# Rounding the feed-forward weights inside the first attention, by sign and comparison

## The reference

```python
def _weight_quant(w):
    scale = 1.0 / jnp.clip(jnp.mean(jnp.abs(w)), 1e-05)
    wq = jnp.clip(jnp.round(w * scale), -1.0, 1.0) / scale
    return w + jax.lax.stop_gradient(wq - w)
def _bitlinear(x, w):
    return jnp.einsum('bsd,fd->bsf', _act_quant(x), _weight_quant(w))
...
x = x + _L0_xattn_ref(_layernorm(x), ctx_512, Wq, Wkv_expand, Wout)
x = x + _L0_ffn_ref(_layernorm(x), W1, W2)      # silu(bitlinear(x, W1)), then bitlinear with W2
x = x + _L1_xattn_ref(_layernorm(x), ctx_512, ...)
x = x + _L1_ffn_ref(_layernorm(x), ...)
```

## Time and profile before

| what | value |
|---|---|
| time, median of 3 runs | 1128.49 us (1125.04 to 1131.27) |
| the profiled execution's own time | 1127.68 us |
| its span, first to last instruction | 1125.9 us |
| busy PE, DVE, ACT, POOL | 88%, 68%, 58%, 25% |
| mean granted TensorE clock | 0.95 of full |

### The profile page before, as it was taken

The page is one execution under the profiler, slowest core; times in us unless marked ns, Lnnn a source line. Parts: engine busy times, 40 slices in busy tenths (PEclk is TensorE's granted clock), DMA queues, the critical chain, the costliest instruction groups (busy, mean ns, idle before and its releaser), DMA issues. The chain is left out here.

```text
span 1125.9 us, 20668 instructions
## 1 busy us (share of the span) xinstructions
PE 994.8 (88%) x7516; PEld 782.9 (70%) x7516; DVE 763.1 (68%) x1654; ACT 651.4 (58%) x1691; POOL 283.4 (25%) x276
## 2 busy tenths in 40 slices
PE   5799999997129999886999999899998999999586
PEld 5678888876014555534888888788887888888485
DVE  6757666664757998435676767577775767777466
ACT  4657777765547878454555555355554555555275
POOL 5765565343033332021001010010101001000372
PEclk9989999999659999987999999999999999999889
DMA  7210000000438000141000000000000000000013
GB/s 263 98 67 6 7 2 2 2 1 1 149 105 249 1 1 2 38 169 57 1 1 19 2 20 2 3 20 1 20 1 23 1 1 1 1 1 2 0 39 113
DMA packets 20091, 41.95 MB, mean 37 GB/s; under 512 B 1168, under 2 KB 4496, under 8 KB 19472
## 3 DMA queue, kind: packets, MB, share of 16 engines
q1 hardware_dynamic: 19984, 40.53, 10.8%
HBM read 36.33 MB, written 4.19 MB: 36 GB/s over the span
## 5 line engine op out<-in xcount | busy, mean ns | idle before, releaser
L1214 POOL TENSOR_TENSOR c_ctx_raw<-c_ctx_raw,c_table 128x1024 f32<-128x1024 f32 x8 | 19.0, 2379 | 448.7 <-PE c_bank_b L1358 366.5
L1440 ACT ACTIVATE probs<-c_score,c_neg_max 128x256 f32<-128x256 f32 x256 | 119.2, 480 | 15.4 <-DVE c_neg_max L1501 15.4
L1426 ACT ACTIVATE c_h<-c_bank_b 128x512 fp32r<-128x512 f32 x64 | 38.3, 598 | 153.6 <-PE c_bank_b L1358 153.6
L559 POOL TENSOR_TENSOR a_probs<-a_probs,a_inv 128x256 f32<-128x256 f32 (+1 forms) x128 | 102.7, 830 | 90.5 <-DVE a_inv L660 90.4
L451 ACT ACTIVATE a_probs<-a_s,a_neg_max 128x128 f32<-128x128 f32 (+1 forms) x256 | 104.4, 435 | 32.3 <-DVE a_neg_max L648 31.9
L1491 DVE TENSOR_TENSOR c_l<-c_bank_b,c_h 128x512 fp32r<-128x512 f32 x64 | 44.3, 692 | 99.2 <-ACT c_h L1426 99.2
L1431 ACT ACTIVATE c_pT_h<-c_turn 128x512 fp32r<-128x512 f32 x128 | 69.9, 596 | 63.4 <-PE c_turn L1348 63.4
L44 PE MATMUL c_acc<-VO_h,c_l 128*128 128x512 f32 x256 | 100.9, 394 | 1.9 <-DVE c_l L1491 1.9
L46 PE MATMUL c_acc<-VO_h,c_h 128*128 128x512 f32 x256 | 100.5, 393 | 0.0
L45 PE MATMUL c_acc<-VO_l,c_h 128*128 128x512 f32 x256 | 100.0, 391 | 0.0
L1501 DVE TENSOR_REDUCE c_neg_max<-c_score 128x2 f32<-128x512 f32 x128 | 82.0, 682 | 9.7 <-PE c_score L1337 8.8
(11 more groups left out here) (253 smaller groups left out, 2866.6 us busy)
## 6 DMA issues: line engine op xcount, KB each, us to landing
w_raw<-in_w SPq DMA_DIRECT2D x1, 4096.0 KB, 13.8
w_raw<-in_w SPq DMA_DIRECT2D x4, 1024.0 KB, 8.8
wq<-in_wq SPq DMA_DIRECT2D x1, 4096.0 KB, 22.8
c_ctx_raw<-in_ctx SPq DMA_DIRECT2D x8, 512.0 KB, 3.6
wo<-in_wo SPq DMA_DIRECT2D x1, 4096.0 KB, 14.3
out<-g_x SPq DMA_DIRECT2D x16, 256.0 KB, 2.1
g_x<-in_x SPq DMA_DIRECT2D x7, 512.0 KB, 6.6
wq_raw<-in_wq SPq DMA_DIRECT2D x4, 256.0 KB, 4.5
```

The source lines that it names most:

```text
L559: last = pool.tensor_tensor(p, p, inv[:, pair, q, :].unsqueeze(2).broadcast_to([P, 2, (q + 1) * P]), ALU.mult)
L1440: last = act.activation(probs[p % 2][:, i, :], score[h][:, t, :], ACT.Exp, bias=neg_max[:, i:i + 1], accum_out=sums[:, i:i + 1])
```

## The change

The rounding stage and the deviations stage ahead of it are gone, and their work moves into the first attention.

- The first weight comes in four transfers instead of one. The second comes in four as well, now inside the attention: they wait in SP's queue until quarters of the first weight have been rounded (`load_w2`), because both use the same memory.
- Sums: ACT takes half of each weight in 4 pieces of 128 x 1024, DVE the other half in 8 pieces of 128 x 512. The matmul with ones becomes a piece of PE's order, once in sequence 2 (ahead of T0) and once in sequence 5 (ahead of proj2), and takes a bank of the rotation. DVE then makes half of the mean, `limit`.
- Rounding: ACT writes Sign(w + limit) in bf16 (8 pieces of 128 x 1024 for each weight), and DVE writes min(w > limit, that) over it (16 pieces of 128 x 512 for each). That gives -1, 0 or 1.
- The pieces stand at fixed places: 4 in each sequence's ACT order, 8 in DVE's (`weights_at`). In DVE's order below, D0 to D7 mark the places of one sequence from 1 on; in ACT's, A0 to A3.
- The deviations for the feed-forward are made on POOL for each sequence, at the end of the next sequence's work (`feed_forward_deviations`), and for the last one at the end of the attention.
- The tensors of the feed-forward and the second attention lie at other places in the store, and the second weight is four tiles instead of one.

```diff
+CH = 4
+ACT_POS, DVE_POS = 4, 8
+SUM_ACT, SUM_DVE, SIGN_AT = (4, 17), (10, 36), (9, 23)
+def quantise_at(i, j):
+    return 20 + j if i == 0 else 47 + j if j < 2 else 48 + j
+def pool_deviations(pool, mv, rstd, var, sq, power, tiles, scale=1.0):
+    ... # the six instructions of deviations(), as a function
+MEANS0 = {(2, 1): ["S1", "pv3'", "proj1", "out0'", "mean0", "T0"], (5, 2): ["S2", "v0", "out1'", "pv0", "mean1", "proj2", "T1"]}
...
+                def load_w2(k):
+                    sp.wait_ge(quantised, 4 * (k + 1))
+                    sp.dma_start(w_raw[1][:, k * F:(k + 1) * F].rearrange("p (c n) -> p c n", c=FC // CH), w_src[1][k]
+                                 ).then_inc(w_in[1][k], DMA)
...
-                sp.dma_start(w1_raw, io["w1"].rearrange("(c p) n -> p c n", p=P)).then_inc(w1_in, DMA)
+                for k in range(CH):
+                    sp.dma_start(w_raw[0][:, k * F:(k + 1) * F], w_src[0][:, k, :]).then_inc(w_in[0][k], DMA)
                 for b in range(4, B):
                     sp.wait_ge(ctx_in, b * DMA)
                     load_context(b)
+                    if b >= B - 2:
+                        load_w2(b - (B - 2))
+                load_w2(2)
+                load_w2(3)
...
+                def add_sums(i, out):                                     # PE
+                    pe.wait_ge(w_summed, i + 1)
+                    pe.matmul(out[:, 0:1], ones[:, :], total[:, i:i + 1], start=True, stop=True).then_inc(crossed, 1)
...
+                def sum_weights(i, j):                                    # ACT
+                    act.activation(thrown, w_raw[i][:, j * 2 * D:(j + 1) * 2 * D], ACT.Abs, accum_out=part[:, i, j:j + 1]
+                                   ).then_inc(act_summed, 1)
+                def sign_weights(i, j):                                   # ACT
+                    if j == 0:
+                        act.wait_ge(limit_ready, i + 1)
+                    if i == 1 and j in (2, 6):
+                        act.wait_ge(quantised, 16 + (4 if j == 2 else 8))
+                    act.activation(quantised_part(i, j * 2 * D, 2 * D), w_raw[i][:, j * 2 * D:(j + 1) * 2 * D], ACT.Sign,
+                                   bias=limit[:, i:i + 1]).then_inc(signed, 1)
+                def weights_at(b, pos):
+                    n = b * ACT_POS + pos
+                    for i in range(2):
+                        if 0 <= n - SUM_ACT[i] < 4:
+                            sum_weights(i, n - SUM_ACT[i])
+                        if 0 <= n - SIGN_AT[i] < 8:
+                            sign_weights(i, n - SIGN_AT[i])
...
+                    else:                                                 # POOL, end of sequence b
+                        feed_forward_deviations(b - 1)
+                feed_forward_deviations(B - 1)
...
+                def sum_weights(i, j):                                    # DVE
+                    dve.tensor_reduce(part[:, i, 4 + j:5 + j], w_raw[i][:, (8 + j) * D:(9 + j) * D], AX.X, ALU.add,
+                                      apply_absolute_value=True)
+                def weight_limit(i):
+                    dve.wait_ge(crossed, i + 1)
+                    dve.tensor_scalar(w_mean[:, i:i + 1], work[bank_of["mean", 0, i]][:, 0:1], 1.0 / (F * D), 1e-5,
+                                      ALU.mult, ALU.max)
+                    dve.drain()
+                    dve.tensor_scalar(limit[:, i:i + 1], w_mean[:, i:i + 1], 0.5, None, ALU.mult)
+                    dve.drain().then_inc(limit_ready, 1)
+                def quantise(i, j):
+                    dve.wait_ge(signed, 8 * i + j // 2 + 1)
+                    q = quantised_part(i, j * D, D)
+                    dve.scalar_tensor_tensor(q, w_raw[i][:, j * D:(j + 1) * D], limit[:, i:i + 1], q, ALU.is_gt, ALU.min
+                                             ).then_inc(quantised, 1)
...
-        inverse_deviations(nc, "bs", mv, rstd, [(w2_raw[:, c * FC // CH:(c + 1) * FC // CH, :], w2_chunks[c], w2_in)
-                                                for c in range(CH)])
-        quantise_weights(nc, w1_raw, w2_raw, w1, w2, mean, w1_in, w2_in)
```

More of the change, by code:

```diff
@@ L167, in steps_of_layer0 @@
         slots = [END0] if b == B else FIRST0 if b == 0 else STEPS0
-        for slot in slots:
-            for x in slot:
+        for n, slot in enumerate(slots):
+            for x in MEANS0.get((b, n), slot):
                 kind, i = x.rstrip("'~+0123"), int(x.strip("'~+")[-1])
@@ L173, in steps_of_layer0, with layer0_attention @@
                     continue
+                if kind == "mean":
+                    own = 0
                 for part in (("TY", "TZ", "TX") if kind == "T" else (kind,)):
                     yield part, own, i
-def layer0_attention(nc, io, X, mv, rstd, ident, identb, store, w1_raw, w1_in):
+def layer0_attention(nc, io, X, mv, rstd, ident, identb, store, w1, w2, w_mean):
     SCALE = float(HD0) ** -0.5
@@ L197, in layer0_attention, with quantised_part @@
         measured, rstd0_ready, y0_ready = m.sem("measured"), m.sem("rstd0_ready"), m.sem("y0_ready")
+        w_raw = [store.place(f"w{i + 1}_raw", 0, [P, CH * F]) for i in range(2)]
+        w_src = (io["w1"].rearrange("(c p) n -> p c n", p=P), io["w2"].rearrange("(k c p) n -> k p c n", p=P, k=CH))
+        w_in = [[m.sem(f"w{i + 1}_in{k}") for k in range(CH)] for i in range(2)]
+        ones, part, total, limit = (m.sb("ones", [P, P]), m.sb("part", [P, 2, 12]), m.sb("total", [P, 2]), m.sb("limit", [P, 2]))
+        thrown = store.place("w_thrown", 25, [P, 2 * D], BF16)
+        ones_ready, act_summed, w_summed, crossed, limit_ready, signed, quantised, restated = (
+            m.sem(n) for n in ("ones_ready", "act_summed", "w_summed", "crossed", "limit_ready", "signed", "quantised", "restated"))
+        def quantised_part(i, start, width):
+            k, at = start // F, start % F
+            flat = w1[:, k, :] if i == 0 else w2[k].rearrange("p c n -> p (c n)")
+            return flat[:, at:at + width]
         y = store.place("y0", 26, [P, TPB, D])
@@ L294, in take_bank @@
                             pe.wait_ge(added, b * TPB + i + 1)
+                        elif kind == "mean":
+                            pe.wait_ge(limit_ready, i + 1)
                         elif kind == "TX":
@@ L407, in _ @@
                         project_out(b, i, out)
+                    elif kind == "mean":
+                        add_sums(i, out)
                     else:
@@ L796, in _ @@
                     invert(b, 3, 0)
+                    weights_at(b, 7)
                     if b == 0:
@@ L962, in step @@
                                 pe.wait_ge(h_copied, 2 * t + 1 + c // HALF)
-                            last = pe.matmul(down[:, :], hqT[:, c, :], w2[:, c, :], start=c == 0, stop=c == FC - 1)
+                            last = pe.matmul(down[:, :], hqT[:, c, :], w2[c // CH][:, c % CH, :], start=c == 0, stop=c == FC - 1)
                         last.then_inc(downed, 1)
```

151 lines of the change are left out of this document (66 added, 85 removed).

## The result

The median goes from 1126.76 us (1121.94 to 1131.27) to 1096.64 us (1091.58 to 1098.15): ratio 0.9725, 95% interval 0.9672 to 0.9779, 2.7% faster. The forecast was 1099.5 us with a range of 1092 to 1110. The profiled execution of the kernel after took 1098.15 us, its span is 1096.4 us, 29.5 us less than the span before.

A forecast was written before the change was run, and what follows sets the result against it. PE bound the attention, but was nearly idle in the removed stretch. 1127.68 - 35.9 + 0 (ACT) + 5.3 (DVE) + 1.7 (matmuls) = 1098.8 us; with 0.8 for the median 1099.6, say 1099.5 us, range 1092 to 1110.

The forecast's parts named there:

- The removed stages: Between attention and feed-forward: 38.92 us go, POOL's last deviations and leaving the block take 3.0 us; gain 35.9 us.
- ACT at nothing: In the attention: 8 Abs and 16 Sign fit ACT's idle times; cost 0 us, upper bound 7 us.
- rival 4: On ACT: Sign isn't in Exp's table set, so table loads cost 41 us, about 1137.5 us; 0.03 together with rival 3.
- The failed step: D4 of sequences 2 and 3: rounding waits for POOL's tile y, starting 1.6 us late; costs 1.6 and 2.2 us.
- the 5.3: In the attention: us lost to DVE's sums and roundings, from overfull idle times and waits for POOL.
- The matmul with ones: In PE's order, sequences 2 and 5: 1.1 us of instructions plus 0.3 us waiting each time; 1.7 us, bounds 1.1 and 4.
- Sequence 7: Last sequence of the attention: D5 waits about 0.5 us for POOL, costing 0.5 us.
- one of the signs that I had named for being wrong: In the profile after: sequences 6 and 7 lengthen as well by over 1 us.
- DVE's pieces, sequences 1 to 6: In the attention before sequence 7: sums and roundings delay PE by 4.8 us, mostly at D4 of sequences 2 and 3.
- rival 1: In the attention: the pieces hide altogether, only the matmuls' 1.1 to 2 us are left; 1094.5 us, chance 0.20.
- Rival 2: In the attention: POOL and DVE block each other, 0.5 us per rounding, 16 us; 1110.5 us, chance 0.20.
- rival 3: In the attention: DVE's queue becomes the bound, pieces cost 56 us; 1150 us, not faster; 0.03 together with rival 4.

The follow-up runs named there:

- the version with both edits: Kernel after, with the last deviations made inside the feed-forward and sequence 7's last three roundings moved behind the last maxima: median 1089.26 us, ratio 0.9657.
- the one with the deviations alone: Kernel before, with only the feed-forward's deviations moved to POOL inside the attention and the rounding stage kept: median 1129.65 us, ratio 1.0021.

## Why the prediction came out

**The removed stages: right.** Predicted 38.9 - 3.0 = 35.9 us, measured 38.92 - 2.95 = 35.97. The three microseconds in their place were the six POOL instructions and 0.42 us for leaving the block.

**ACT at nothing: right, and shown by leaving the pieces out.** Abs 1.09 us (predicted 1.15), Sign 1.18 us (1.15). The groups of ACT between 60 and 290 us hold no table load, with 16 Signs between 224 exponentials, so rival 4 is excluded.

**The failed step: a rounding that comes beside the tile y waits until POOL is done with it.** I put D4 of sequences 2 and 3 at 1.6 us late, and 3.8 us of the 5.3 rest on it. Two pairs of rows, each a tile and the rounding beside it, in sequences 2 and 3 of the kernel after:

```profile
109.09 2.08 POOL L641 TENSOR_SCALAR y<-g_x,g_mean_var,g_rstd 128x512 f32<-128x512 f32 x1 [0.18 <-issue]
...
109.69 0.72 DVE L811 SCALAR_TENSOR_TENSOR w<-w_raw,a_limit,w 128x512 bf16<-128x512 f32 x1
...
140.23 2.08 POOL L641 TENSOR_SCALAR y<-g_x,g_mean_var,g_rstd 128x512 f32<-128x512 f32 x1 [0.18 <-issue]
...
140.56 0.98 DVE L811 SCALAR_TENSOR_TENSOR w<-w_raw,a_limit,w 128x512 bf16<-128x512 f32 x1
```

One that comes 0.60 us into the tile takes 0.72 us, the least there is; one that comes 0.33 us into it takes 0.98. The tile took 2.08 us both times. The rule was taken from L625 beside POOL's multiplications, and beside those it holds: D5 of sequence 2 took 1.01 us beside two of them.

```profile
112.86 2.06 POOL L650 TENSOR_TENSOR a_probs<-a_probs,a_inv 128x256 f32<-128x256 f32 x2
113.01 1.01 DVE L811 SCALAR_TENSOR_TENSOR w<-w_raw,a_limit,w 128x512 bf16<-128x512 f32 x1
```

I carried it over to another POOL instruction, for which I had no row. Measured is 0.55 us in sequence 2 without its matmul, and 0.2 in sequence 3, where I had 1.6 and 2.2. Sequence 2's 0.55 is of another origin (the sums beside the first statistics). Sequence 3's 0.2 lies in slot 3, behind D4 to D6, where I had looked for it (6.84 us, 6.67 without DVE's pieces, 6.60 with one input).

**The matmul with ones: nearly five times too large.** 0.16 us in sequence 2 and 0.20 in sequence 5, 0.36 against 1.7. I had booked the 1.1 us of the group and 0.3 us of waiting, twice; the slots that hold it show neither in full. Part of it is the clock at which that row was taken: 0.51 in the removed stretch, where an instruction took 355 ns; in the attention, at full clock, the same four took 234.

```profile
L451 PE MATMUL a_work<-a_total,a_ones 128*128 128x1 f32 x4 | 0.7, 234 | 0.0
```

**Sequence 7: half a microsecond predicted, 2.1 measured.** D5 took 1.01 and D6 0.92 us there, ahead of the last maxima, which came 2.0 us later behind their S. Moving three roundings behind these maxima took 1.9 us of it away. That PE covers such a delay in the steady sequences with its pieces of the next one, and has none left in the last, is my reading of its order. It was one of the signs that I had named for being wrong: sequence 7 with its tail is longer by over 1 us for the pieces' sake, while sequence 6 isn't (30.10 us against 30.12).

| term | predicted | measured |
|---|---|---|
| stages removed | -35.9 | -35.97 |
| ACT's pieces | 0 | 0 |
| DVE's pieces, sequences 1 to 6 | 4.8 | 0.7 (2 to 6) |
| DVE's pieces, sequence 7 and tail | 0.5 | 2.1 |
| matmuls with ones | 1.7 | 0.36 |
| what is left between the two profiled executions, the clock above all | 0 | +3.3 |
| sum | -28.9 | -29.5 |

The last entry is what is left of 29.5 us: +0.3 at the start, -1.5 in sequences 0 and 1, +1.05 in sequence 7, +0.85 in the tail, +2.6 behind the first tile. All but the start's lie in stretches whose granted clock was below 1.00, and each is of a size by which kernels differ that have the same instructions there. So the forecast was close partly by luck: my costs were 3.8 us too high (7.0 against 3.2), and these differences put 3.3 us in. By the medians it is the same, a gain of 30.1 us where 29.0 were forecast and the terms as measured give 32.8.

**The rivals.** The pieces' cost of 3.2 us lies between rival 1 (up to 2) and my forecast (5 and more); in sequences 2 to 6, where it was argued, rival 1 was the nearer. Rival 2, 16 us of blocking, isn't there: taking the second input away gave under 1 us in the trace. It and rival 3 show what lies beyond: with the roundings doubled 16 us of the gain are lost.

**What stays open.** Why the granted clock falls to half where it does, once in sequence 7 and once not, with the same instructions; whether a version that gives PE less idle time in the tail changes that; why the matmuls with ones show 0.36 us of their 0.7; and why the medians of the version with both edits and of the one with the deviations alone lie further off than their stretches say (by 3 us each).

## What to carry to other kernels

A stage of elementwise work on its own can vanish into the idle gaps of a matmul-bound stage ahead of it, if it is cut into pieces as long as the gaps, and if its one serial point (here the mean) comes early enough. Count the gap behind each place in every kind of sequence, the first and the last above all: in sequences 2 to 6 DVE's pieces cost 0.7 us, in the last one two ahead of the last maxima cost 2. Where the last iteration has no successor, move the pieces behind its chain.

## What the runs showed of the hardware

How long a DVE instruction with two SBUF inputs is held up depended here on the kind of POOL's instruction, not only on its length. Roundings that began during one of POOL's multiplications (TENSOR_TENSOR) took 0.92 to 1.39 us, and multiplications of 128 x 256 up to 1.16 us in place of 0.61; roundings that began just ahead of one took their 0.72. During a TENSOR_SCALAR of 2.08 us they took 0.72 and 0.98. The Trainium skill, page "SBUF — State Buffer", section "Who interferes with whom", says that a DVE instruction with two SBUF inputs contends with a GpSimd instruction that reads SBUF, and that the shared ports are an exclusive lock; elsewhere that page gives the lock to the first of the two for the whole instruction, and so had I taken it. The multiplications agree. The TENSOR_SCALAR doesn't, and the measurement decides. The kernel that rounds twice shows it from the other side, in sequence 2: its tile began beside a rounding and took 0.3 us longer, and the second rounding took 0.4 us longer and still ended 0.8 us before the tile.

```profile
117.61 0.74 DVE L812 SCALAR_TENSOR_TENSOR w<-w_raw,a_limit,w 128x512 bf16<-128x512 f32 x1
118.38 1.14 DVE L815 SCALAR_TENSOR_TENSOR w<-w_raw,a_limit,w 128x512 bf16<-128x512 f32 x1
...
117.91 2.38 POOL L642 TENSOR_SCALAR y<-g_x,g_mean_var,g_rstd 128x512 f32<-128x512 f32 x1 [1.98 <-PE a_work L383]
```

The same times come again in its sequence 3, and its second roundings at D4, which began 1.36 and 1.34 us into the tile, took 0.75 us. All of these pairs fit a tile that blocks for about its first 0.6 us (an estimate from their times); no run varied the tile itself, so why is open.

The granted clock fell to the lower of its two levels (1.2 and 2.4 GHz) at differing places in executions of the same kernel. Inside the attention it fell in the first two sequences, in sequence 7 and in the tail, never in sequences 2 to 6. In sequence 7 PE waits between pieces, busy for 16.91 of 20.55 us at full clock; in sequence 3 for 30.37 of 30.71. Sequence 7 took 20.55, 22.06, 23.11 or 24.54 us at a mean granted clock of 1.00, 0.92, 0.85 or 0.79, the last of these in the kernel whose roundings have one input:

```profile
243.63:268.17 24.54, 20.92 (x206) 16.02 (x206) 14.83 (x33) 16.59 (x61) 11.48 (x19) 0.79 0.01 2
```

Differences of 2 us between medians of this kernel, whose runs spread over 6 to 11 us in a group, are of this size; the stretches at full clock tell them apart, the medians don't.
